# Moving the divide and the residual add of a relational attention layer from VectorE to GpSimd

## The reference

```python
weights = jax.nn.softmax(rel_w)
for r in range(3):
    h = (x @ W[r]).reshape(N, 4, 32)
    score = leaky_relu(a_s[src] + a_d[dst], 0.2)        # per head
    score = where(edge_type == r or self loop, score, -1e9)
    ex = exp(score - segment_max(score, dst)[dst])
    denom = segment_sum(ex, dst)
    rel_out = segment_sum((ex / denom[dst])[:, :, None] * h[src], dst)
    out = out + weights[r] * (rel_out + bias[r])
x = layernorm(x + out)
```

## Time and profile before

| | us |
|---|---|
| median of 3 runs | 2529.91 |
| the runs | 2530.45, 2518.57, 2529.91 |
| the profiled execution, its own time | 2515.76 |
| its span (first to last instruction) | 2514.0 |
| VectorE busy in the span | 2044.0 (81%) |
| TensorE matmul busy, spans that overlap | 2138.6 (85%) |
| ScalarE busy | 1777.3 (71%) |
| GpSimd busy | 123.6 (5%) |

### The profile page before, as it was taken

The page is one execution under the profiler, slowest core; times in us unless marked ns, Lnnn a source line. Parts: engine busy times, 40 slices in busy tenths (PEclk is TensorE's granted clock), DMA queues, the critical chain, the costliest instruction groups (busy, mean ns, idle before and its releaser), DMA issues. The chain is left out here.

```text
span 2514.0 us, 89498 instructions
## 1 busy us (share of the span) xinstructions
PE 2138.6 (85%) x34234; PEld 1884.3 (75%) x34234; DVE 2044.0 (81%) x4438; ACT 1777.3 (71%) x3000; POOL 123.6 (5%) x158
## 2 busy tenths in 40 slices
PE   4999999799799799596967989888998899969846
PEld 4655555699699699495966989878997888959724
DVE  7999999788788787616169999899999999976863
ACT  5999999766666666202048999789997999937622
POOL 2111111000000000000001000000000000001500
PEclk8999999899899899798988999999999999979968
DMA  4355555543342342281812333223321333125200
GB/s 108 157 209 209 209 209 209 197 133 104 95 142 91 106 143 79 67 261 66 262 66 62 102 102 89 68 76 102 112 85 51 101 109 102 43 74 165 90 0 26
DMA packets 178874, 294.15 MB, mean 117 GB/s; under 512 B 6383, under 2 KB 158834, under 8 KB 178590
## 3 DMA queue, kind: packets, MB, share of 16 engines
q1 hardware_dynamic: 177802, 288.86, 34.8%
q0 software_dynamic: 800, 1.26, 0.2%
HBM read 205.62 MB, written 84.47 MB: 115 GB/s over the span
## 5 line engine op out<-in xcount | busy, mean ns | idle before, releaser
L1175 ACT ACTIVATE relmsk<-relad,relthr 125x625 bf16 (+1 forms) x1080 | 770.9, 810 | 19.7 <-DVE relsel L1232 19.0
L1382 PE MATMUL ps<-relmv,relsel 125*128 125x66 f16 x15000 | 736.5, 197 | 34.2 <-DVE relsel L1232 28.5
L1382 PEld LDWEIGHTS ps<-relmv,relsel 125*128 125x128 f16 x15000 | 685.2, 100 | 52.0 <-DVE relsel L1232 30.7
L1386 PE MATMUL ps<-relmv,relct 125*128 125x132 f16 x3750 | 544.1, 229 | 2.6 <-issue 2.5
L1232 DVE TENSOR_TENSOR relsel<-relmsk,relct 125x1920 f16<-125x1920 bf16 (+1 forms) x375 | 424.3, 1131 | 12.4 <-ACT relmsk L1175 12.4
L1227 DVE SCALAR_TENSOR_TENSOR relsel<-relad,relthr,relct 125x625 f16<-125x625 f16 (+1 forms) x420 | 359.5, 865 | 8.1 <-DVE relnum L1261 4.7
L453 ACT ACTIVATE stage<-ps 125x375 f32 x625 | 314.1, 604 | 38.2 <-PE ps L393 33.9
L346 DVE TENSOR_SCALAR col<-iota_col,window_col 125x376 bf16<-125x376 f16 x1250 | 311.2, 326 | 3.5 <-PE ps L393 3.5
L393 PE MATMUL ps<-col,lo 125*125 125x375 bf16 x1250 | 291.0, 345 | 17.5 <-DVE col L346 17.0
L1386 PEld LDWEIGHTS ps<-relmv,relct 125*128 125x128 f16 x3750 | 246.5, 99 | 2.7 <-issue 2.7
L393 PEld LDWEIGHTS ps<-col,lo 125*125 125x125 bf16 x1250 | 136.9, 139 | 145.2 <-DVE col L346 142.1
(11 more groups left out here) (480 smaller groups left out, 2872.0 us busy)
## 6 DMA issues: line engine op xcount, KB each, us to landing
counts<-stage SPq DMA_DIRECT2D x75, 800.0 KB, 4.8
ct<-counts_all SPq DMA_DIRECT2D x75, 800.0 KB, 4.6
relct<-counts SPq DMA_DIRECT2D x75, 800.0 KB, 4.7
counts_all<-total SPq DMA_DIRECT2D x25, 800.0 KB, 7.3
stage<-counts_all SPq DMA_DIRECT2D x25, 800.0 KB, 4.5
g1ct<-counts_all SPq DMA_DIRECT2D x25, 800.0 KB, 4.6
g2ct<-counts_all SPq DMA_DIRECT2D x25, 800.0 KB, 4.6
relad<-ad_rows SPq DMA_DIRECT2D x12, 1250.0 KB
```

What stands on the lines that cost most here:

```text
L1175: act.activation(msk[:, s % 5, n, :, 0:P], ad[:, bass.ds(g % 2, 1), h] .rearrange("p a (b d) -> p (a b) d", d=PAD)[:, :, 0:P], ACT.Relu, b ...
L1382: pe.matmul(K.ps[:, b, 2 * h * F:2 * (h + 1) * F], sel[:, s % 5, h, b], vs[:, (h * 2 + p) * 2 * F:(h * 2 + p + 1) * 2 * F], start=False, s ...
L1386: ins = pe.matmul(K.ps[:, b, 0:2 * HF].rearrange("p (h a f) -> p h a f", h=H, a=2)[:, :, 1], ct[0:P, s // 5, b, s % 5], vs[:, (4 + p) * HF ...
```

## The change

GpSimd takes over `divide` and `add`. VectorE keeps `divisors` and `weights` behind steps 3 and 4 (`BEHIND = (0, 1)`). In a loop over the five turns GpSimd waits for the weights, multiplies `num` by `rden`, waits for its own result, and adds onto `x`. The semaphore `w.divided` now counts two a turn instead of three, and a new one, `w.weighted`, stands between the two GpSimd instructions. VectorE's waits for `w.added` ahead of `drain`, and at the end of a relation, are as before. The wait for `biased` moves from VectorE to GpSimd. The arithmetic is the same.

```diff
-    BEHIND = (0, 1, 2, 3)
+    BEHIND = (0, 1)
...
@@ gpsimd, in the loop over the relations
+                        pool.wait_ge(biased, 2)
+                    with pool.Fori(0, 5) as g:
+
+                        pool.wait_ge(w.divided, 2 * g + 2)
+                        pool.tensor_tensor(num[:, :, :, 0:32], num[:, :, :, 0:32],
+                                           rden[:].unsqueeze(3).to_broadcast([P, 5, H, 32]), ALU.mult).then_inc(w.weighted, 1)
+                        pool.wait_ge(w.weighted, g + 1)
+                        own = x4[:, bass.ds(5 * g, 5)]
+                        pool.tensor_tensor(own, own, num[:, :, :, 0:32], ALU.add).then_inc(w.added, 1)
...
@@ vector
-                        v.wait_ge(w.divided, 3 * g + 1)
+                        v.wait_ge(w.divided, 2 * g + 1)
                         v.tensor_scalar(rden[:], rden[:], wr, Q.top[:], ALU.mult, ALU.mult).then_inc(w.divided, 1)
-
-                    def divide(g):
-
-                        v.wait_ge(w.divided, 3 * g + 2)
-                        v.tensor_tensor(num[:, :, :, 0:32], num[:, :, :, 0:32],
-                                        rden[:].unsqueeze(3).to_broadcast([P, 5, H, 32]), ALU.mult).then_inc(w.divided, 1)
-
-                    def add(g):
-
-                        v.wait_ge(w.divided, 3 * g + 3)
-                        own = x4[:, bass.ds(5 * g, 5)]
-                        v.tensor_tensor(own, own, num[:, :, :, 0:32], ALU.add).then_inc(w.added, 1)
...
-                    if r == 0:
-                        v.wait_ge(biased, 2)
...
-                                (divisors, weights, divide, add)[BEHIND.index(s - AHEAD)](g - 1)
+                                (divisors, weights)[BEHIND.index(s - AHEAD)](g - 1)
...
                     drain(4)
                     divisors(4)
                     weights(4)
-                    divide(4)
-                    add(4)
                     if r < R - 1:
                         v.wait_ge(w.added, 5)
```

More of the change, by code:

```diff
@@ L1111, in layer_heads @@
             w.landed = [S(f"r{r}_landed{c}") for c in range(5)]
-            (w.adst, w.ad_landed, w.masked, w.used, w.full, w.scaled, w.drained, w.mready, w.turns, w.divided, w.added) = (
+            (w.adst, w.ad_landed, w.masked, w.used, w.full, w.scaled, w.drained, w.mready, w.turns, w.divided, w.weighted, w.added) = (
                 S(f"r{r}_" + n) for n in ("adst", "ad_landed", "masked", "used", "full", "scaled", "drained", "mready",
-                                          "turns", "divided", "added"))
+                                          "turns", "divided", "weighted", "added"))
             rel.append(w)
@@ L1323, in relation @@
                         if s - AHEAD in BEHIND:
-                            (divisors, weights, divide, add)[BEHIND.index(s - AHEAD)](3)
+                            (divisors, weights)[BEHIND.index(s - AHEAD)](3)
                     v.wait_ge(w.added, 4)
```

## The result

The changed kernel takes 2530.43 us (median of 20 runs), the kernel before 2520.68 us (20 runs, the three of the table among them). The ratio of the fast runs is 1.005 with a 95% interval of 1.0034 to 1.0067: slower by 0.5%, about 12.6 us by the ratio and 9.8 us by the medians. The profiled execution has a span of 2527.7 us, 13.7 us more than before. Six of the changed kernel's twenty runs lie at 2539.8 to 2547.7 us and the others at 2527.7 to 2531.8; of the kernel before, one lies at 2547.95 and the others at 2515.6 to 2530.7. The direction was forecast. The size, +21.8 us, was not met. The time of 2530.4 us lies in the stated range, 2528 to 2564 us, near its lower edge; the forecast of 2552 us stood besides on a median of three runs that lay 9.2 us above that of twenty.

What follows compares the result with a forecast made beforehand. VectorE was taken to bound the turns. Removed work -17.8, stops +30.7, absorbed -1.1, relation ends +4.7 and reductions +5.3 gave +21.8 us on 2529.9, thus 2552 us, range 2528 to 2564 us.

Steps and rivals of the forecast that it cites:

- The stops of VectorE: In the turns, each of GpSimd's two instructions stops a VectorE step 1.28 us: +30.7 us over 12 turns.
- the line through 1024 and 3200 values: Sizing of GpSimd's instructions from two measured ones: 1.54 us for 640 values.
- GpSimd gets in at the first boundary: Behind the weights, GpSimd's multiply starts when the running L1227 ends and holds up L1232.
- The 1.1 us to be absorbed: Last turn of the first relation: VectorE's 4.45 us wait for TensorE absorbs the net loss, -1.1 us.
- The ends: From the weights to L736 at each relation's end, GpSimd's two instructions take 1.56 us more: +4.7 us for three.
- The reduction: The reduction over partitions behind relations 1 and 2 starts 2.6 us late from GpSimd's configuration change: +5.3 us.
- L329's 7.2 us: Time from a configuration change to GpSimd's instruction L329, taken as the change's duration ahead of the reduction.
- as far up as the median before: The new median was expected 14.2 us above the profiled execution, like the old one; base 2529.9 us.
- No exclusion: Rival, chance 0.09: GpSimd reads between VectorE's accesses and stops no steps; -7.8 us, 2522 us.
- A share: Rival, chance 0.12: steps stretch 0.38 us for each microsecond of GpSimd; +6.2 us, 2536 us.
- No gap: Rival, chance 0.12: GpSimd gets in only when VectorE stands still ahead of the drain; +31.1 us, 2561 us.
- It would all count: In the turns, the whole 17.8 us removed from VectorE would shorten them, since ScalarE's 51.3 us lie below 52.8 us.

Runs made afterwards that it cites:

- nothing: Changed kernel with the divide and the add left out, GpSimd only passing the semaphores on: profiled span 2511.2 us.
- memsets: Changed kernel with the divide and the add left out, GpSimd writing constants in three memsets a turn instead: span 2519.7 us.
- copies: Changed kernel with the divide and the add left out, GpSimd copying 512 values a partition from `num` twice a turn instead: span 2515.1 us.
- one more: Changed kernel plus one more GpSimd multiply a turn, of 512 values a partition into an unread array: 2538.0 us.
- the run with GpSimd behind the reduction: Changed kernel, but GpSimd finishes the fifth turn's multiply and add behind the next relation's reduction over partitions: 2521.4 us.

## Why the prediction was right in direction and wrong in size

*The stops of VectorE.* The mechanism was right: steps are stopped, twice a turn, by GpSimd's reads and by nothing else (nothing, memsets, copies, one more). The size was 30.7 us and is 12 x 2.25 = 27.0 us. The failing step is the line through 1024 and 3200 values, which gave 1.54 us for each instruction; the multiply takes 1.26 to 1.27 and the add 1.42 us. The stop is GpSimd's time less 0.18 to 0.27 us (1.01 of 1.27, 1.24 of 1.42, 0.85 of 1.05, 0.35 and 0.41 of 0.62), as the 0.26 us reckoned. That GpSimd gets in at the first boundary was wrong for eleven of twelve multiplies, without a price.

*What was removed.* 1.48 us a turn, as the run with nothing in their place shows in its first two turns (51.76 and 52.80 us against 53.22 and 54.25).

*The turns together.* -17.8 + 27.0 = +9.2 us, and the twelve turns are together 9.2 us longer. The 1.1 us to be absorbed in the last turn of the first relation do not show in that sum. That turn is 0.99 us shorter than before instead of 0.78 longer, with a granted clock of TensorE of 0.93 in it and 0.90 before. In the third relation the opposite happened: 51.01 us, 1.83 more, at 0.93 instead of 0.97. These and smaller ones in the second relation cancel; why the grants differ stays open. That the sum comes out so well is in part luck.

*The ends.* 4.7 us forecast. From the divisors on, L736 comes 1.24 and 1.26 us later and the layer norm 1.30 us: 3.8 us. Again the duration on GpSimd. The third of them did not reach the end of the program: from the last drain to there are 304.1 us before and after. Where it came back was not followed; 2.5 us count.

*The reduction.* 5.3 us forecast, 1.40 and 1.26 us: 2.7 us. The failing step was to take L329's 7.2 us, a change in the other direction, for this one. Toward the reduction it takes 5.6 to 6.1 us (5.96 and 5.76 here, 5.58 to 6.06 in four experiments), toward an ordinary instruction 7.1 to 9.2 us (7.12 and 7.88 in the run with GpSimd behind the reduction, 8.13 to 9.16 ahead of the large add in nine traces). The Trainium skill's 5.95 us (GPSIMD Engine Reference, Instruction dispatch), which I had set aside, is right for this direction.

*The sum.* +9.2 us in the turns, +2.5 at the ends, +2.7 for the reductions, and a layer that began 0.6 us earlier make 13.8 us, with a span 13.7 us longer. Against the forecast +21.8 the stops were sized 3.7 us too large, the reductions 2.6 and the ends 2.2: by one duration that was too long and by a configuration change read in the wrong direction. The 1.1 us counted as absorbed went the other way. The medians differ by less still, 9.8 us, since the profiled execution of before was one of its faster ones.

*The base.* The step "as far up as the median before" failed too. The 14.2 us between the profiled execution and the median of three did not come back: twenty runs of before have their median 4.9 us above its 2515.76 us, those of the changed kernel 1.0 us above the 2529.45 us of the profiled one.

*The rivals.* No exclusion is excluded by the 2.25 us. A share came nearer in the time (+6.2 us forecast), but the trace is against it: a stop has nearly GpSimd's whole length. No gap is excluded: no drain waits for GpSimd. What no rival had is TensorE as the bound in the later turns as soon as VectorE is relieved. The last paragraph of the prediction named it as a sign of being wrong, but "It would all count" for the removed 17.8 us looked at ScalarE's slack alone; TensorE's 50.1 us of work and its 3.4 us of waiting at each boundary leave less than 1 us of the 54.25. It did not touch the result, because the turns grew. It would have swallowed the gain, had the stops not been there.

## What to carry to other kernels

Work moved to an idle GpSimd is not free beside a VectorE whose instructions read two arrays in SBUF: each GpSimd instruction that reads costs VectorE its duration less about 0.2 us (0.18 to 0.27 in five cases), and with 1.26 and 1.42 us against the 0.74 us on VectorE itself the move loses. Put such work where VectorE waits for someone else, where the two stops, 2.25 us together, cost nothing, or leave it on VectorE in those same gaps. Before a saving is booked on the engine that bounds, look at the next engine's time in the same turn, its waits and the clock that it is granted included. And give a changed order on GpSimd the 6 to 9 us of each change of configuration, or put idle time behind the change: with 47 and 49 us there it cost nothing.

## What the runs showed of the hardware that was not expected

- A GpSimd instruction that waits for a busy VectorE may let one more VectorE instruction pass: 2.87 to 2.89 us in eleven turns, 1.84 us in one, for the same instruction at the same place, with nearly the same total stop (2.25 and 1.07 + 1.17 = 2.24 us). What decides between the two stays open: in both the multiply was issued 0.17 us behind the start of an L1236.
- The time from a configuration change to the next instruction depends on the direction: 5.6 to 6.1 us toward the reduction over partitions, 7.1 to 9.2 us toward an elementwise instruction. With 47 and 49 us between the change and the reduction nothing of it was seen.
- 21 us less of VectorE's busy time (2022.8 against 2044.0) were worth 2.8 us of span, none of it in the twelve turns: TensorE, with its wait at each turn's start and a granted clock below 1 behind most of them (0.60 in the window above), has no slack in the later turns. What the clock alone costs there was not measured.
